# One issuer instead of two for the adjacency tiles: all four quarters of each tile loaded by SyncE

## The reference, cut to what matters

```python
h = jnp.maximum(_layernorm(x, axis=-1), 0.0)
x = x + _L0_gnn_ref(h, adj, L0_gnn_weight, L0_gnn_bias)      # hyperbolic layer: adj @ x_tangent
h = jnp.maximum(_layernorm(x, axis=-1), 0.0)
x = x + _L1_gnn_ref(h, L1_gnn_context, adj, L1_gnn_W_common, L1_gnn_w_left, L1_gnn_b_left, ...)

# the heart of _L0_gnn_ref
support_t = adj @ x_tangent                                   # (4096,4096) @ (4096,128), float32
# the heart of _L1_gnn_ref: attention over the edges of adj
logits = left[:, None] + right[None, :]
logits = jnp.where(logits >= 0, logits, 0.2 * logits)
logits = jnp.where(adj_tensor <= 0.0, -jnp.inf, logits)
x = jax.nn.softmax(logits, axis=-1) @ relation
```

## Time and profile before

| | |
|---|---|
| three runs | 556.97, 557.08, 557.21 us; median 557.08 us |
| profiled execution | 554.63 us, its span 552.8 us |
| phase 1, first to last product of PE with `adj` | to 291.9 us of the span |
| granted TensorE clock, mean | 0.965 of full speed |
| bytes moved by queue | q1 (SP) 48.64 MB, q10 (ACT) 31.20 MB, q0 (POOL) 4.35 MB |

### The profile page before, as it was taken

One profiled execution on the slowest core, in us unless ns is written; L12 is line 12 of the kernel. 1 busy time (PEld: TensorE's weight loads), 2 busy tenths in 40 slices (PEclk: granted clock), 3 DMA queues, 4 the chain that ended last, 5 costly groups with the idle time before them and its releaser, 6 DMA issues.

```text
span 552.8 us, 9390 instructions
## 1 busy us (share of the span) xinstructions
PE 480.3 (87%) x3209; PEld 413.2 (75%) x3209; DVE 447.1 (81%) x907; ACT 314.0 (57%) x466; POOL 271.7 (49%) x348
## 2 busy tenths in 40 slices
PE   1733879999999999999994777899999999999995
PEld 1622758877787788888883556788888888888884
DVE  3997878777787798888888899968788787878763
ACT  1584767748586778686866632535353535353521
POOL 6840899999999675535357996202020202020200
PEclk9985999999999999999997879999999999999998
DMA  7899999999999999998970000110101010101010
GB/s 171 186 234 223 252 300 301 275 280 266 311 289 320 260 332 320 338 293 218 273 194 20 22 18 28 32 40 20 39 18 41 13 46 8 52 2 38 1 39 20
DMA packets 91851, 84.75 MB, mean 153 GB/s; under 512 B 7552, under 2 KB 89728, under 8 KB 91808
## 3 DMA queue, kind: packets, MB, share of 16 engines
q1 hardware_dynamic: 56032, 48.64, 35.4%
q10 hardware_dynamic: 33424, 31.20, 20.5%
q0 software_dynamic: 2352, 4.35, 2.9%
HBM read 79.96 MB, written 4.21 MB: 152 GB/s over the span
## 4 chain that ended last, share of the span: by engine, by line
PE 54%; POOL 24%; DVE 7%; SPq 7%; issue 3%; DMA 3%; ACT 2%; ACTq 0%; POOLq 0%; DVEq 0%
PE ps L749 35%; PE ps L716 19%; POOL mask L501 8%; POOL mask L492 7%; SPq L382 3%; SPq L299 2%; DVE room L1234 2%; DMA mask<-in_L_gnn_context_dram 2%; DVE room L1201 2%; SPq L373 2%; DVE room L1185 1%; POOL out_dram L589 1%; POOL post L559 1%; POOL xk L596 1%; DVE room L1208 1%
## 5 line engine op out<-in xcount | busy, mean ns | idle before, releaser
L716 PE MATMUL ps<-room 128*128 128x256 f32 x1024 | 227.9, 382 | 28.5 <-DVE room L1117 22.7
L749 PE MATMUL ps<-room 128*128 128x258 f16 x2048 | 232.3, 276 | 20.5 <-POOL room L629 15.0
L749 PEld LDWEIGHTS ps<-room 128*128 128x128 fp8e4 x2048 | 200.5, 98 | 52.3 <-issue 16.0
L716 PEld LDWEIGHTS ps<-room 128*128 128x128 f32 x1024 | 193.4, 191 | 60.6 <-DVE room L999 27.5
L871 ACT ACTIVATE mask<-room,constants 128x1024 int8<-128x1024 f32 x128 | 146.1, 1145 | 59.0 <-DVE room L999 56.3
L999 DVE STREAM_TRANSPOSE room<-room 128x512 f32<-128x512 f32 x184 | 124.5, 697 | 19.8 <-PE ps L716 11.2
L643 POOL TENSOR_TENSOR h_room<-h_room 128x512 f32<-128x512 f32 x7 | 8.9, 1275 | 146.3 <-DVE post L1275 146.3
L1201 DVE SCALAR_TENSOR_TENSOR room<-mask,constants,room 128x512 int32<-128x512 int32 x64 | 64.5, 1007 | 10.8 <-ACT room L919 10.8
L919 ACT ACTIVATE room<-relu_u,r_col 128x512 int8<-128x512 f32 x64 | 42.0, 713 | 40.6 <-PE ps L749 40.6
L919 ACT ACTIVATE room<-room,r_col 128x512 int8<-128x512 f32 x62 | 40.9, 712 | 34.5 <-PE ps L749 34.5
L999 DVE STREAM_TRANSPOSE room<-mask 128x512 f32<-128x512 f32 x72 | 48.9, 697 | 8.6 <-PE ps L716 4.2
(11 more groups left out here) (160 smaller groups left out, 343.1 us busy)
## 6 DMA issues: line engine op xcount, KB each, us to landing
room<-in_adj_dram SPq DMA_DIRECT2D x100, 256.0 KB, 7.6
room<-in_adj_dram ACTq DMA_DIRECT2D x84, 256.0 KB, 8.3
mask<-in_adj_dram SPq DMA_DIRECT2D x40, 256.0 KB, 8.1
mask<-in_adj_dram ACTq DMA_DIRECT2D x32, 256.0 KB, 9.0
mask<-in_L_gnn_context_dram SPq DMA_DIRECT2D x16, 256.0 KB, 11.7
xk<-in_x_dram POOLq DMA_DIRECT2D x32, 64.0 KB, 6.4
out_dram<-xk POOLq DMA_DIRECT2D x32, 64.0 KB, 4.8
h_room<-out_dram SPq DMA_DIRECT2D x32, 64.0 KB, 2.4
```

The lines of the kernel that those rows point to most:

```text
L716: mm = pe.matmul(acc[parity][:, h], xt[:, tangent_order.index(blocks_of(c, k)[j]), :], turned[:, k % TSLOTS, j * (CH // 2):(j + 1) * (CH / ...
L749: mm = pe.matmul(ps[:, 2 * t + w, 0:GW], part[slot(c, g)][:, kk, t * P:(t + 1) * P], G[w][:, k, :], start=(k == 0), stop=(k == NK - 1))
```

## The change

`load_tile` is called for all four quarters by SP, in the order 0, 1, 2, 3, for every tile, the first six included. ACT's calls and the list `behind` are gone. SP's wait for the slot is the one that was there.

```diff
@@ -185,8 +185,6 @@
         before = [max([u for u in range(t) if slot_of[u] == n], default=None) for t, n in enumerate(slot_of)]
-        behind = [min([u for u in range(t + 1, len(slot_of)) if slot_of[u] == n], default=None)
-                  for t, n in enumerate(slot_of)]
@@ -390,7 +388,7 @@
                     if before[t] is not None:
                         sp.wait_ge(block_turned, L * (before[t] + 1))
-                    load_tile(sp, c, g, LOW if t >= len(loaded) else (0, 2, 1, 3))
+                    load_tile(sp, c, g, range(NQ))
@@ -877,10 +875,6 @@
                     if half in steps:
                         steps[half]()
-                    if half % HALVES == HALVES - 1:
-                        tile = behind[c * NC + half // HALVES]
-                        if tile is not None:
-                            load_tile(act, tile // NC, tile % NC, HIGH)
```

## The result

| | before | after |
|---|---|---|
| runs | 556.60 to 557.28 us, median 557.08 (5) | 605.81 to 621.74 us, median 612.42 (5) |
| ratio of the compared runs | | 1.095, 95% interval 1.092 to 1.099 |
| profiled execution | 554.63 us, span 552.8 | 617.12 us, span 615.3 |
| last product with `adj` | 291.9 us | 352.5 us |

The change makes the kernel 55 us slower in the median; 620.5 us was predicted, range 598 to 635. Five runs of the changed kernel lie 2.6% apart, those of before 0.1%. The ratio rests on the three runs from 605.81 to 612.42 us; the profiled execution is one of the two slower ones, so its trace explains 62.5 us and not 55.

A forecast was written before the change was run, and what follows sets the result against it. PE's chain bounds phase 1 until a lone queue slows the loads to 226 GB/s; phase 1 then ends at 355.5 in place of 291.9 us, +63.6, making 618.2 us profiled and 620.5 us forecast, range 598 to 635.

The forecast's parts named there:

- What bounds the kernel before: Phase 1: PE's chain, 3.45 us a tile, is the path only while loads reach about 290 to 304 GB/s.
- 226 GB/s, last landing at 350.5 us, phase 1 over at 355.5 us (+63.6): Phase 1 loads: 66.37 MB by the lone queue take 293.7 us, +0.8 at the start, 5.0 us behind the last landing.
- The median from the profiled execution: Whole kernel: profiled execution 618.2 us, the median 2.45 us above it, 620.7 us.
- The reading of the lone queue: Loads: a single quarter of 32 partitions fills at some 225 to 240 GB/s; more takes quarters in different halves side by side.
- +0.8 us for the order at the start: Start: the first 16 quarters, 4.19 MB, go at 226 and not 236 GB/s, 18.6 for 17.8 us.
- ACT's freed issues 0: Phase 1: ACT loses 116 issues, 54 us in all, mostly off the chain; value 0, bounds 0 to -2 us.
- SP's added issues 0: Phase 1: SP gains 116 issues, four taking 1.8 us of a tile's 3.45; value 0, bounds 0 to +2.
- Rival A: Phase 1 loads: a lone queue with 6 slots ahead reaches 240 to 280 GB/s; 581.5 us, range 570 to 603; chance 0.12.
- B: Phase 1: PE, now pausing between tiles, is granted the low clock for much of it; 648 us; chance 0.05.
- C: Loads: the number of queues doesn't matter, q1 alone carries 290 GB/s, PE stays the path; 557 us; chance 0.05.
- D: Phase 1: one queue is enough, as the rival before, and ACT's freed time shows; 555.5 us; chance 0.03.
- PE's idle time +60 us, DVE's wait for DMA 60 us: Phase 1: DVE waits for DMA by some 60 us in all, and PE's idle time rises by as much.

The follow-up runs named there:

- e4: Changed kernel, but from tile 6 on each of SP's DMAs loads only half of the rows, part of the computation on old data; ratio 1.0030 to the kernel before.
- e9: Kernel before, both queues, only the first six tiles in the order 0, 1, 2, 3 in place of 0, 2, 1, 3; ratio 1.0018.
- e1: Changed kernel, SP alone, but every tile's quarters in the order 0, 2, 1, 3; 571.81 to 600.37 us, median 589.0 beside 555.6.
- e2: Kernel before, both queues, but SP issues quarters 0 and 2, ACT 1 and 3; ratio 1.035, without the last run of 600.08 us.
- e3: Kernel before, but ACT issues quarter 3 ahead of quarter 2; ratio 1.0006, 555.20 to 556.91 us.
- e12: Changed kernel with half of the rows from tile 6 on, but the first six tiles in the old order 0, 2, 1, 3; ratio 1.0012 to the kernel before.
- e6: Changed kernel, SP alone, but tiles from other source blocks, still four DMAs of 32 partitions in order; 610.83 to 615.13 us, ratio 1.104 to the kernel before.
- e5: SP alone as in the changed kernel, but other source blocks, one 1 MB DMA of 128 partitions per tile; ratio 1.025 to the kernel before, without the fourth run.

## Why the prediction was right, point by point

- **What bounds the kernel before**, and that 290 to 304 GB/s are needed: held. DVE waits for DMA as soon as less arrives.
- **226 GB/s, last landing at 350.5 us, phase 1 over at 355.5 us (+63.6):** measured 230 GB/s, last landing at 347.6 us and last product at 352.5 us (+60.6) in the profiled execution. The 5.0 us behind the last landing held (4.9); the size was off by 3 us in the rate. I let q0's bytes displace q1's; here q1 alone runs at 222 GB/s (80 to 110 us), and the slices of the page at 235 to 242 go with q0's traffic, so a part of q0's bytes came on top.
- **The median from the profiled execution:** I put it 2.45 us above, as before; it was 4.70 us below. These 7.15 us and the 1.1 us by which the profiled execution missed 618.2 are the 8 us between forecast and median. I did not foresee that runs bound by the lone queue would lie 2.6% apart. The agreement of the one profiled execution to 1.1 us is therefore in part luck; that every run fell into the range is not.
- **The reading of the lone queue.** I ascribed 226 against 236 to 238 GB/s to the order of the quarters and doubted it for the clock. The changed kernel takes the doubt away: its first tiles, with the clock at 1.00 and the order 0, 1, 2, 3, run at this rate.
```profile
20.00:34.00 14.00, 8.45 (x63) 7.20 (x62) 13.97 (x54) 9.24 (x18) 13.08 (x18) 1.00 1.11 218
```
  Over all traces this stretch had 216 to 220 GB/s with the order 0, 1, 2, 3 (changed kernel, e4, e9) and 226 to 236 with 0, 2, 1, 3 (before, e1, e2, e3, e12). So the order counts, but the 236 of the kernel before was the top of a spread of 10.
  The wording "quarters 0 and 2, or 1 and 3, side by side" was too narrow (e3), and "whatever the source" held (e6). What I put down to queues out of step, 223 and 229 GB/s with both queues loaded, is not explained: SP's and ACT's quarters are in different halves there too, and both queues moved alike (0.55 MB by q1, 0.54 by q10 from 106 to 111 us). These stretches are also no measurement of a lone quarter, as which the prediction set them beside 218 GB/s.
- **+0.8 us for the order at the start:** as a term of the transfers it is absorbed; as a later start of GpSimd it is 1.25 us in the kernel where nothing else changed (e9), of which up to 0.9 us may be spread.
- **ACT's freed issues 0, SP's added issues 0:** held within what can be measured (e12, with e4). SP's wait for DVE shrank to 9.8 us, its issues took 1.07 us and a quarter landed 10.0 to 10.2 us after its issue, as forecast.
- **Rival A** (240 to 280 GB/s) is what e1, with another order, did; with the order of the change it did not come. **B:** did not come: the mean granted clock was 1.00 from 84 to 187 us, 0.98 to 292 us and 0.96 to 340 us. **C and D:** false for this change, though e5 shows that their idea, one queue is enough, nearly holds when a DMA fills all partitions (274 GB/s, 1.025 of the time before).
- **PE's idle time +60 us, DVE's wait for DMA 60 us:** wrong in how it is split. PE's idle time ahead of its products rose from 28.5 to 69.0 us and its busy time from 227.9 to 248.0 us; the two together are the +60.6 us. A busy time of pipelined products is modelled and takes in short gaps. DVE waited 100.8 us for DMA, more than the 60 by which phase 1 grew, since its waits at that line for PE and ACT turned into it: 24.8 us before, 2.2 us for PE and none for ACT after.
- **Phase 2 unchanged:** 262.8 in place of 260.9 us from the last product to the end, 1.9 us that were not forecast and were not tried by an experiment.

## What to carry to other kernels

Before one issuer is made to do the work of two, look for a stretch of the trace in which that issuer was alone with a full queue: its GB/s, set against the GB/s that the path needs, gave this result to within 1.5%. One queue with DMAs over 32 or 64 neighbouring partitions carried 226 GB/s here, with DMAs over 128 it carried 274; either fill all 128, or let two queues fill one half each. Where a load gates a long chain of another engine, the order of the loads ahead of it can count too.

## What the runs showed that I had not expected

- Two queues that both change halves from quarter to quarter moved 278 GB/s, one such queue 247 (e2 and e1, 187 to 280 us); two queues that keep to one half each moved 291.
- With SP alone and the order 0, 2, 1, 3 the same kernel took from 571.8 to 600.4 us, and its rate went from 237 (86 to 116 us) to 279 GB/s (280 to 300 us) within one execution; the kernel before stayed within 0.7% over all its runs.
- One DMA of 1 MB over 128 partitions had a DMA share of 0.97 at 274 GB/s, the small ones 1.12 at 226: the share says that the engines are occupied, not how much they move.
